# First feed-forward of a decoder: the residual by VectorE in pairs of batches, in place of identity products

## The reference

```python
def _L0_ffn_ref(x, gate_w, down_w, down_b, up_w, up_b):   # 8 experts, 64 hidden each
    gate = softmax(x.mean(axis=1) @ gate_w.T)             # one choice per batch
    top_w, top_i = top_k(gate, 2)
    top_w = top_w / (top_w.sum(-1) + 1e-8)
    h = gelu(x @ down_w[top_i] + down_b[top_i]) * top_w
    return h @ up_w[top_i] + (top_w * up_b[top_i]).sum()
...
x = _layernorm(x + _L0_ffn_ref(x, ...))                   # computed here
x = _layernorm(x + _L1_attn_ref(x, ...))                  # begins with a layernorm of its own
```

## Time and profile before

| | us |
|---|---|
| median of 3 runs | 418.78 |
| the runs | 417.75 to 419.29 |
| the profiled execution, its own time | 420.02 |
| its span from the first to the last instruction | 418.20 |
| outside the span | 1.82 |
| mean granted clock of TensorE, share of 2.4 GHz | 0.979 |

### The profile page before, as it was taken

One profiled execution on the slowest core, in us unless ns is written; L12 is line 12 of the kernel. 1 busy time (PEld: TensorE's weight loads), 2 busy tenths in 40 slices (PEclk: granted clock), 3 DMA queues, 4 the chain that ended last, 5 costly groups with the idle time before them and its releaser, 6 DMA issues.

```text
span 418.2 us, 9993 instructions
## 1 busy us (share of the span) xinstructions
PE 381.3 (91%) x4008; PEld 258.8 (62%) x4008; DVE 273.0 (65%) x704; ACT 234.4 (56%) x442; POOL 130.5 (31%) x126
## 2 busy tenths in 40 slices
PE   4989996798999999999999999899998999999991
PEld 2556683566766847566667778446776466666671
DVE  6778877535657586779898885634666544444446
ACT  2855568656677267889999971235556432222210
POOL 6939932101331330028789780100012000000001
PEclk9999999869999999999999999999999999999998
DMA  6320000000000000112323210720000000000001
GB/s 178 80 52 2 4 2 2 2 2 2 5 1 2 0 2 2 63 56 78 105 84 112 77 38 2 241 61 3 3 4 2 0 2 0 0 2 1 2 0 50
DMA packets 16881, 13.84 MB, mean 33 GB/s; under 512 B 6548, under 2 KB 14133, under 8 KB 16837
## 3 DMA queue, kind: packets, MB, share of 16 engines
q1 hardware_dynamic: 15538, 12.51, 10.1%
q10 hardware_dynamic: 1299, 0.71, 0.6%
HBM read 12.64 MB, written 0.57 MB: 32 GB/s over the span
## 4 chain that ended last, share of the span: by engine, by line
PE 78%; ACT 9%; DVE 7%; issue 3%; DMA 1%; POOL 0%; POOLq 0%; DVEq 0%; ACTq 0%
PE PS L1923 10%; PE PS L1993 7%; PE PS L1494 7%; PE PS L1997 7%; PE PS L2024 6%; PE PS L1434 5%; PE PS L1910 4%; PE PS L1473 4%; PE PS L1514 4%; ACT att L655 3%; PE PS L1440 2%; PE PS L1566 2%; PE PS L1724 2%; PE PS L1429 2%; PE PS L1497 2%
## 5 line engine op out<-in xcount | busy, mean ns | idle before, releaser
L655 ACT ACTIVATE att<-PS 77x512 f32<-77x512 f32 (+1 forms) x96 | 51.6, 591 | 43.5 <-PE PS L1497 43.5
L982 DVE TENSOR_REDUCE mxp<-PS 128x4 f32<-128x308 f32 (+1 forms) x96 | 48.0, 536 | 32.3 <-PE PS L1473 32.2
L902 ACT ACTIVATE kM<-PS 128x512 f32<-128x512 f32 x32 | 19.1, 597 | 55.5 <-PE PS L1993 54.4
L511 POOL TENSOR_TENSOR rstd<-ve,neg_half 128x1 f32<-128x1 f32 x24 | 14.0, 585 | 108.3 <-DVE ve L976 108.3
L1306 DVE TENSOR_TENSOR_SCAN big<-big,PS 128x768 f32<-128x768 f32 x22 | 38.3, 1748 | 6.1 <-PE PS L1910 5.7
L1373 DVE TENSOR_TENSOR big<-kM,PS 128x512 f32<-128x512 f32 x32 | 21.9, 687 | 27.3 <-PE PS L1997 26.1
L505 POOL TENSOR_TENSOR rstd<-ve,neg_half 128x4 f32<-128x4 f32 x6 | 6.2, 1030 | 102.5 <-DVE ve L932 102.5
L1993 PE MATMUL PS<-xT,V 128*128 128x512 f32 x64 | 33.0, 596 | 1.1 <-DVE xT L1361 0.8
L1997 PE MATMUL PS<-xT,V 128*128 128x512 f32 x64 | 32.7, 592 | 0.0
L2024 PEld LDWEIGHTS PS<-big 128*128 128x128 f32 x256 | 29.7, 192 | 3.3 <-issue 3.3
L2024 PE MATMUL PS<-big 128*128 128x128 f32 x256 | 29.7, 275 | 0.0
(11 more groups left out here) (362 smaller groups left out, 862.5 us busy)
## 6 DMA issues: line engine op xcount, KB each, us to landing
kM<-Cdram SPq DMA_DIRECT2D x6, 384.0 KB, 3.5
XH<-Cdram SPq DMA_DIRECT2D x5, 384.0 KB, 3.5
xT<-Cdram SPq DMA_DIRECT2D x5, 384.0 KB, 3.3
V<-in_L_ffn_Wg SPq DMA_DIRECT2D x1, 1024.0 KB, 5.5
V<-in_L_ffn_Wu SPq DMA_DIRECT2D x1, 1024.0 KB, 8.1
out_x<-X SPq DMA_DIRECT2D x2, 256.0 KB, 2.3
ctxN<-in_ctx ACTq DMA_DIRECT2D x1, 308.0 KB
X<-in_x SPq DMA_DIRECT2D x1, 256.0 KB, 3.8
```

Of the source, the lines that this page charges most:

```text
L655: A_(PT[0:nk, i % 2, g], bank4(at.bank("exp", i, g), nk), ACT.Exp, scale=at.scale)\
L982: V_.tensor_reduce(mxp[:, b % 3, g, 0:J], PS[:, at.bank("max", b, g), 0:J * nk].rearrange("p (j k) -> p j k", j=J), axis=AX.X, op=ALU.max) ...
```

## The change

- Both identity products go (`residual`).
- The up products go by pairs of batches p = 0 to 3, each pair in a bank of its own (up.0 to up.3 in banks 4, 5, 6 and 7), 256 columns used. Per batch: the bias, then its four slices. Each pair waits until all its slices are scaled.
- VectorE scales `hid` in three groups of batches, 0 and 1, 2 and 3, 4 to 7: eight instructions of 256 columns and four of 512, in place of eight of 512.
- VectorE adds x (`X[0]`) to each pair's bank and writes the sum into `R` in SBUF, four instructions of 256 columns. This releases the bank. Statistics and all norms then read `R`.
- v5.0 and k5.1 now have up.2 and up.3 before them in their banks, in place of cexp and cT.

```diff
--- before.py
+++ after.py
@@ -169,7 +169,7 @@
 ACT_FIRST = {"x0T.0": 2, "ctxT.0": 0, "x0T.1": 3, "ctxT.1": 1, "k1.0": 2, "k1.1": 7, "kv.0": 6, "kv.1": 5, "kv.2": 6, "kv.3": 6}
 DVE_FIRST = {"q1.0": 4, "q1.1": 5, "v1.0": 6, "v1.1": 4}
 ACT_OWN = {**ACT_FIRST, "x1T.0": 3, "k2.0": 0, "k2.1": 4, "x1T.1": 6}
-DVE_OWN = {**DVE_FIRST, "q2.0": 1, "q2.1": 6}
+DVE_OWN = {**DVE_FIRST, "up.2": 6, "up.3": 7, "q2.0": 1, "q2.1": 6}
 Q2T_BANK = 2
 ACT_JOBS = (list(ACT_FIRST)
             + ["x1T.0", "k2.0", "k2.1", "x1T.1"]
@@ -177,7 +177,7 @@
             + ["W5T", "k5.0", "xnT.0", "xnT.1", "router.0", "router.1", "srow.0", "srow.1", "XI.0", "v5.1"] + [f"XI.{b}" for b in range(1, B)]
             + ["x4T.0", "x4T.1", "q5.0", "q5.1", "x5T.0"])
 DVE_JOBS = (list(DVE_FIRST) + ["q2.0", "q2.1"]
-            + ["logits8", "cexp", "cT", "up.0", "up.1", "v5.0", "k5.1", "scol"]
+            + ["logits8", "cexp", "cT", "up.0", "up.1", "up.2", "up.3", "v5.0", "k5.1", "scol"]
             + ["rank", "cumU", "dposA.0", "dposA.1", "dposS.0", "dposS.1", "dl.0", "dl.1", "x5T.1", "logits6"])
 
 
@@ -1178,40 +1178,38 @@
         V_.tensor_copy(cexp[:], PS[:, take("cexp"), 0:4 * B].rearrange("p (t b) -> p t b", t=4)).then_inc(dring.copied, 1)
         V_.tensor_copy(cT[0:E0], PS[0:8, take("cT"), 0:8]).then_inc(dring.copied, 1)
         dve.wait_ge(dring.copied, dring.emptied)
-        for c in range(2):
+        for lo, hi in ((0, 2), (2, HB), (HB, B)):
             for t in range(4):
-                aring.wait_copied(dve, f"hid.{t}.{c}")
-                v = hid[:, t, c * 512:(c + 1) * 512].rearrange("p (b n) -> p b n", b=HB)
-                V_.tensor_tensor(v, v, wide(cexp[:, t, c * HB:(c + 1) * HB], [128, HB, T]), ALU.mult)\
-                    .then_inc(event("hid_scaled"), 1)
-
-
-        ups = []
-
-        def summed(b):
-            return PS[:, ups[b // HB], (b % HB) * D:(b % HB + 1) * D]
-
-        for c in range(2):
+                aring.wait_copied(dve, f"hid.{t}.{lo // HB}")
+                v = hid[:, t, lo * T:hi * T].rearrange("p (b n) -> p b n", b=hi - lo)
+                V_.tensor_tensor(v, v, wide(cexp[:, t, lo:hi], [128, hi - lo, T]), ALU.mult).then_inc(event("hid_scaled"), 1)
+
+
+        for p in range(B // 2):
+            c, q = p // 2, slice(2 * p, 2 * p + 2)
             h = slice(c * HB, (c + 1) * HB)
-            ups.append(take(f"up.{c}"))
-            for b in range(c * HB, (c + 1) * HB):
-                ins = V_.bn_stats(st[:, b, :], summed(b))
-            step(ins)
-            for b in range(c * HB, (c + 1) * HB):
-                ins = V_.bn_aggr(mv[:, b, :], st[:, b, :])
-            step(ins)
-            step(V_.tensor_scalar(ve[:, h], mv[:, h, 1], EPS, None, ALU.add))
-            V_.scalar_tensor_tensor(ve4[:, h], ve[:, h], EPS, mv[:, h, 1], ALU.mult, ALU.add).then_inc(event("ve4_ready"), 1)
+            i = take(f"up.{p}")
+            V_.tensor_tensor(R[:, q], X[0][:, q], PS[:, i, 0:2 * D].rearrange("p (b n) -> p b n", b=2), ALU.add)\
+                .then_inc(dring.copied, 1)
+            dve.wait_ge(dring.copied, dring.emptied)
+            for b in (2 * p, 2 * p + 1):
+                ins = V_.bn_stats(st[:, b, :], R[:, b, :])
+            if p % 2:
+                step(ins)
+                for b in range(c * HB, (c + 1) * HB):
+                    ins = V_.bn_aggr(mv[:, b, :], st[:, b, :])
+                step(ins)
+                step(V_.tensor_scalar(ve[:, h], mv[:, h, 1], EPS, None, ALU.add))
+                V_.scalar_tensor_tensor(ve4[:, h], ve[:, h], EPS, mv[:, h, 1], ALU.mult, ALU.add).then_inc(event("ve4_ready"), 1)
         for c in range(2):
             dve.wait_ge(event("rstd4_ready"), c + 1)
             for b in range(c * HB, (c + 1) * HB):
-                ins = V_.tensor_scalar(XH[:, b, :], summed(b), mv[:, b, 0:1], rstd4[:, b:b + 1], ALU.subtract, ALU.mult)
+                ins = V_.tensor_scalar(XH[:, b, :], R[:, b, :], mv[:, b, 0:1], rstd4[:, b:b + 1], ALU.subtract, ALU.mult)
             ins.then_inc(event("xh4"), 1)
         for c in range(2):
             dve.wait_ge(event("rstd4_ready"), 2 + c + 1)
             for b in range(c * HB, (c + 1) * HB):
-                ins = V_.tensor_scalar(X[1][:, b, :], summed(b), mv[:, b, 0:1], rstd[:, b:b + 1], ALU.subtract, ALU.mult)
-            ins.then_inc(dring.copied, 1)
+                V_.tensor_scalar(X[1][:, b, :], R[:, b, :], mv[:, b, 0:1], rstd[:, b:b + 1], ALU.subtract, ALU.mult)
 
 
         V_.tensor_copy(V5[:, 0:HB, :, 0:HD], bank4(take("v5.0"), NC).rearrange("p b (h d) -> p b h d", h=H)).then_inc(dring.copied, 1)
@@ -1694,14 +1692,6 @@
         pe.wait_ge(event("pooled"), 2)
         product(dring, "logits8", pooledT[:], gate3T[:], 8, 8)
         cexp_bank, cT_bank = fill(dring, "cexp"), fill(dring, "cT")
-        ups = []
-
-        def residual(c):
-
-            ups.append(fill(dring, f"up.{c}"))
-            M_(PS[:, ups[c], :], ident[:], flat(half(X[0], c)), start=True, stop=False)
-
-        residual(0)
         hidden(1, (0, 1))
         pe.wait_ge(event("c8_ready"), 1)
         for e in range(E0):
@@ -1710,19 +1700,16 @@
                      c8[:, e:e + 1].to_broadcast([B, BN]), ident[0:B, 0:B], start=True, stop=True)
         ins.then_inc(dring.full, 1)
         nc.tensor.transpose(PS[0:8, cT_bank, 0:8], c8[:], ident[0:8, 0:8]).then_inc(dring.full, 1)
-        residual(1)
         hidden(1, (2, 3))
         dring.wait_copied(pe, "cT")
-        for c in range(2):
-            for b4 in range(HB):
-                M_(PS[:, ups[c], b4 * D:(b4 + 1) * D], cT[:, c * HB + b4:c * HB + b4 + 1].to_broadcast([128, 128]), upb3[:],
-                   start=False, stop=False)
-            for t in range(4):
-                pe.wait_ge(event("hid_scaled"), 4 * c + t + 1)
-                for b4 in range(HB):
-                    b = c * HB + b4
-                    ins = M_(PS[:, ups[c], b4 * D:(b4 + 1) * D], hid[:, t, b * T:(b + 1) * T], up3T[:, t, :],
-                             start=False, stop=t == 3 and b4 == HB - 1)
+        for p in range(B // 2):
+            i = fill(dring, f"up.{p}")
+            pe.wait_ge(event("hid_scaled"), 4 * min(p, 2) + 4)
+            for k in range(2):
+                b = 2 * p + k
+                M_(PS[:, i, k * D:(k + 1) * D], cT[:, b:b + 1].to_broadcast([128, 128]), upb3[:], start=True, stop=False)
+                for t in range(4):
+                    ins = M_(PS[:, i, k * D:(k + 1) * D], hid[:, t, b * T:(b + 1) * T], up3T[:, t, :], start=False, stop=t == 3)
             ins.then_inc(dring.full, 1)
```

## The result

| | before | after |
|---|---|---|
| median, us (14 executions of each) | 418.71 | 416.39 |
| lowest of them | 417.22 | 414.82 |
| ratio, 95% interval | | 0.9948 [0.9933, 0.9963] |
| the profiled execution, its own time | 420.02 | 416.11 |
| its span | 418.20 | 414.3 |

One of the fourteen executions of the kernel before took 644.66 us; the median does not feel it. The gain is 2.3 us where 1.09 were forecast. The profiled executions differ still more, by 3.9 us. The first question is therefore where in the span these 3.9 us are. Parts of the page of the changed kernel come first: its span, the granted clock in 40 slices of it, and the chain by engine.

A forecast was written before the change was run, and what follows sets the result against it. TensorE, 78% of the last-ending chain, was taken as the bound. The terms -1.05 + 0.05 + 0.0 - 0.09 = -1.09 us took the profiled run from 420.02 to 418.9 and the median to 417.7, range 416.8 to 419.3.

The forecast's parts named there:

- Part 1: First identity product, ahead of c8 on TensorE: removing it gains nothing, since the wait for c8 covers it.
- Part 2: Second identity product, on TensorE's chain behind c8: removing it saves its whole 1.05 us.
- Part 3: Up products by pairs on TensorE: same count and pace, 2.23 us a pair, no extra time.
- Part 4: TensorE's wait for VectorE's scaling before pair 0: costs 0.05 us, between 0 and 0.2 (later bounds 0 to 0.3).
- Part 5: VectorE's four adds of x after the up products: only the last pair counts, cost 0.0 us, bounds 0 and 0.4.
- Part 6: Norms into XH read from SBUF: faster, but ScalarE's copy of xnT.0 then holds router.0, so 0.09 us gained.
- Part 7: v5.0 and k5.1 wait for up.2's and up.3's adds in the bank ring: margin 2 us, cost 0.
- the fall at 175.7 is spared: Rival: the shift moves a 3.4 us stretch at 1.2 GHz elsewhere, up to 1.7 us less, 416.0; chance 0.08.
- VectorE became no bound: Rival: 128x256 scalings cost as much as 128x512, so TensorE waits; +0.3 us, 419.1; chance 0.06.
- The clock did not fall in the stage: Rival: TensorE's clock falls for 3.4 us within 128 to 142; +0.6 us, 419.4; chance 0.10, 0.03 for a longer fall.
- POOL's power beside XH's norms: Rival: POOL's second power waits for the first half's four norms from SBUF; gain 0.37, time 418.4; chance 0.05.
- the rule weighed against part 6: Skill's rule: VectorE in two-port mode and GpSimd lock each other out, putting POOL's power behind the norms; rows show at most 0.03 us.

The follow-up runs named there:

- bias_first: The changed kernel with each pair's first bias product ahead of its wait for the scaling, and waits slice by slice: median 416.19 us, ratio 0.9946 to before.
- identity_kept: The changed kernel with both identity products put back at their old places as work nobody reads: median 417.36 us, ratio 0.9992 to before.
- dense2_before: The kernel before with seven dummy products added in TensorE's pause at 82 us only: median 415.20 us, ratio 0.9937 to before.
- delay_small: The changed kernel with two dummy products (0.43 us) between the last up product and W5T's transposes: median 417.10 us, ratio 0.9982 to before.

## Why the prediction missed

**The bound (right).** TensorE was the chain, and what left the stage left the span: 0.73 to 0.76 us in the stage, with the rest of the kernel unchanged but for its clock.

**Part 1, the first identity product (right).** Nothing forecast, nothing found: 17.79 against 17.78.

**Part 2, the second (mechanism right, 0.19 us too large).** The forecast took the 1.05 us of the chain's row. It measured 0.86, two passes of 0.43. The first product behind the pause had 0.19 us on top of that pace; take it away and the next has them. This is also why the up products ended only 0.74 us earlier against c8, and not the 1.05 that the prediction gave as a sign. The row for this was in the same view, 1.72 for the four passes behind it.

**Part 3, the pairs (right).** Pair ends are 10 x 0.223 apart, with 0.22 and 0.89 alternating in the chain.

**Part 4, pair 0's wait (right in kind, 0.05 forecast, 0.13 measured).** The weight load at 130.76 stood idle for 0.69 us, and bias_first takes 0.13 back. The twelve scalings took 5.18 us, the 256-column ones 0.34 from start to start where 0.32 was taken. It lies within the stated bounds of 0 to 0.3.

**Part 5, the adds (right).** The last add takes 0.42 us, and the add with two statistics stands in the place of four statistics; identity_kept, with all the adds, has the stage of before.

**Part 6, the norm from SBUF (0.09 forecast, nothing found).** XH's eight norms took 2.36 us, as forecast, and xnT.1 follows xnT.0 without a gap. But ScalarE's copy of xnT.0, for which 0.69 us was taken, takes 0.79 on the chain. It took as long before (from 146.64), and ended 0.05 us ahead of router.0's start both times, so it held router.0 before as well.

**Part 7, the new waits in the ring (right).** v5.0 and k5.1 did not wait.

With the measured sizes the sum is -0.86 + 0.13 + 0 + 0 = -0.73 in place of -1.09. The stage shows -0.73 by the router's product, and the comparison at equal clock -0.87 with 0.25 either way. The sum promised 0.36 us too much, and that error goes the other way from the miss.

**The step that failed is the one that turned the sum into a median and a range: it put the clock's share in the difference at nothing.** By the line at equal clock that share was 1.1 us, from a mean clock of 0.9826 to one of 0.9866, more than the edited code gave. The offset of 1.24 us between the profiled run and the median was carried over as if it were a constant, and the spread of 417.75 to 419.29 as if it were noise about it. Both are mostly the number of clock falls in an execution: the profiled run, at 0.979, was of a poor group, and an edit can move executions between the groups. The rival "the fall at 175.7 is spared" had the right sign and nearly the right price (1.4 us measured in the profiles, up to 1.7 said), but it had a chance of 0.08, with the argument that nothing in the change aims at it. Nothing has to: in dense2_before seven products at 82 us are enough, and delay_small says the same of two at 140 us, with twelve executions to go by. It also looked only at the fall behind the stage and not at the two ahead of it. The range should have gone two falls down and one up, about 415 to 419. The chance of 0.88 for a change within 0.5% had the same fault; the measured ratio, 0.9948, lies on that line. (A slip beside it: 418.4 and 0.8 make 419.2 for the upper end, not 419.3.)

**The other rivals.** VectorE became no bound (the add of the last pair waited 1.29 us for TensorE). The clock did not fall in the stage in any profile. POOL's power beside XH's norms took 1.05 us, against 1.01 and 1.04, so that rival is refuted for XH. The last power, beside the norms into X[1], took 1.13 us where it took 1.01 before, the sign that the prediction had set at 1.1; it is off the path.

## What to carry to other kernels

When a kernel's executions differ by a per cent, look up the granted clock of each before a sum is set against the median: the spread may be a few falls of the clock, each with a price (here about 1.1 us in the mean), and an edit can change their number far from where it stands. Compare stages between fixed places of two profiles and not whole spans; here the stage repeated to 0.01 us while the span of one and the same program varied by 3.7. And when an instruction goes from behind a pause, credit its pace (here 0.43 us a pass), not the length that the chain gives it, which holds 0.19 us for being the first.

## What the runs showed of the hardware

**VectorE beside POOL.** The norms into X[1] read SBUF now and took 3.25 us for eight, where the same eight took 2.36 for XH. One of them explains it (columns: minimum, median and maximum in ns, first and last start):

```profile
L1212 DVE TENSOR_SCALAR X<-R,mv,rstd x8: 334/346/1277, 144.0 to 146.8; 128x128 f32<-128x128 f32 x8
```

The windows of these norms alone show which (length, busy, and how many instructions touch the window), and the timeline of POOL what ran beside it:

```profile
144.75:145.10 0.35, 0.35 (x3) 1.00 0.00 0
145.10:145.45 0.35, 0.35 (x1) 1.00 0.00 0
145.45:145.80 0.35, 0.35 (x1) 1.00 0.00 0
145.80:146.15 0.35, 0.35 (x1) 1.00 0.00 0
146.15:146.50 0.35, 0.35 (x2) 1.00 0.00 0
```

```profile
144.87 1.32 POOL L594 TENSOR_TENSOR kM<-Wqkvo,colmask 128x512 f32<-128x512 f32 x1
```

One single norm fills 145.10 to 146.15. It began 0.13 us behind POOL's 128x512 product (L594, in SBUF) and ended 0.09 behind it, 1.28 us in place of 0.34. It repeats in every profile of a kernel with these norms (1.27 to 1.28 us). POOL's powers of 128x4, which ran beside the other norms, held up none of them. Before, with the same product beside them (147.18 to 148.45), none of the eight norms from PSUM took over 0.404. The Trainium skill, "SBUF — State Buffer", section "Who interferes with whom", says that against a VectorE instruction that takes both port pairs, whichever of the two issues first keeps the shared ports for its whole instruction. This trace agrees, with VectorE as the one that waits. So the rule weighed against part 6 did bite, in the eight norms that have slack (VectorE still waited 1.00 us before scol) and through another instruction of POOL than the power. An estimate from 1.28 - 0.34: had a product like L594 stood beside XH's norms, up to 0.9 us would have been on the path.

**Dummy work and the clock.** Seven products without use (1.62 us of the chain in dense2_before) raised the mean granted clock of the whole execution from 0.983 to 0.992 and took 0.63% off the time, with no instruction of the arithmetic changed, and no profile with them has a fall between 81 and 90, where all twelve others have one; eight at another thin place gained nothing. Why the one place works and the other does not is not shown by these runs.
